# Keys and gathers of a graph-convolution kernel with matmuls of 256 columns in place of 512

## The reference, cut to what matters

```python
x_flat = x.reshape(B, C, N).transpose(0, 2, 1)          # B, C, N = 4, 128, 1024
emb = jnp.einsum('bnc,ec->bne', x_flat, dist_w)         # 32 wide
d2 = sq[:, :, None] + sq[:, None, :] - 2.0 * jnp.einsum('bne,bme->bnm', emb, emb)
_, idx = jax.lax.top_k(-dist, K)                        # K = 24
adj = (knn_mask & (dist <= THRESHOLD)) | jnp.eye(N, dtype=bool)[None]
S = (adj_f / De[:, None, :]) @ adj_f.transpose(0, 2, 1) / Dv[:, :, None]
out_flat = S @ X_lin + x_flat                           # then batch norm and SiLU
```

## Time and profile before

| | before |
|---|---|
| time, median of 3 runs | 173.44 us (173.38 to 173.76) |
| profiled execution, time | 173.33 us |
| profiled execution, span of the instructions | 171.5 us |
| TensorE matmul busy | 153.0 us, 89% |
| VectorE busy | 143.8 us, 84% |
| ScalarE busy | 118.5 us, 69% |
| GpSimd busy | 105.7 us, 62% |

### The profile page before, as it was taken

The page is one execution under the profiler, slowest core; times in us unless marked ns, Lnnn a source line. Parts: engine busy times, 40 slices in busy tenths (PEclk is TensorE's granted clock), DMA queues, the critical chain, the costliest instruction groups (busy, mean ns, idle before and its releaser), DMA issues.

```text
span 171.5 us, 4076 instructions
## 1 busy us (share of the span) xinstructions
PE 153.0 (89%) x1237; PEld 98.7 (58%) x1237; DVE 143.8 (84%) x863; ACT 118.5 (69%) x199; POOL 105.7 (62%) x160
## 2 busy tenths in 40 slices
PE   6999989899989999899999989999999899999000
PEld 2334523445556765566666757667877778979000
DVE  0676999999999894999999999599769986688582
ACT  1257679998696996985578799649916575590590
POOL 1000556869984677499996479999619999380000
PEclk9999999999999999999999999999999999999955
DMA  5821000406628666309726070980641369993057
GB/s 192 260 115 2 2 4 0 63 4 122 90 38 176 87 53 114 74 16 198 124 40 122 5 122 6 212 155 6 122 91 38 61 185 95 155 343 153 0 209 281
DMA packets 42346, 17.72 MB, mean 103 GB/s; under 512 B 38832, under 2 KB 39496, under 8 KB 42320
## 3 DMA queue, kind: packets, MB, share of 16 engines
q1 hardware_dynamic: 41456, 17.03, 47.3%
q10 hardware_dynamic: 864, 0.40, 0.9%
HBM read 6.11 MB, written 2.13 MB: 48 GB/s over the span
## 4 chain that ended last, share of the span: by engine, by line
PE 76%; ACT 6%; POOL 6%; DVE 6%; issue 4%; ACTq 0%; DVEq 0%; POOLq 0%
PE pt L500 23%; PE pg L474 21%; PE po L533 10%; PE pt L562 6%; PE po L453 3%; PE po L431 3%; PE pt L533 2%; PE po L440 2%; POOL x_wide L845 2%; DVE xn L1173 2%; ACT key L715 2%; POOL tw L837 1%; ACT xn L801 1%; PE pg L555 1%; PE pg L453 1%
## 5 line engine op out<-in xcount | busy, mean ns | idle before, releaser
L983 DVE MAX8 cand<-key 128x8 f32<-128x64 f32 x512 | 78.1, 208 | 1.4 <-ACT key L715 1.1
L500 PEld LDWEIGHTS pt<-xp,H 128*128 128x128 bf16 x768 | 44.4, 97 | 8.6 <-issue 7.6
L500 PE MATMUL pt<-xp,H 128*128 128x128 bf16 (+1 forms) x768 | 49.1, 220 | 0.0
L715 ACT ACTIVATE key<-pg 128x512 f32<-128x512 f32 x64 | 34.6, 594 | 19.1 <-PE pg L474 18.7
L474 PE MATMUL pg<-right,left 64*128 64x512 f32 x128 | 40.1, 641 | 2.4 <-ACT key L715 2.4
L882 POOL TENSOR_SCALAR H<-sign 128x1024 bf16<-128x1024 bf16 x32 | 33.4, 1044 | 13.1 <-ACT sign L723 13.1
L723 ACT ACTIVATE sign<-key,thr 128x1024 bf16<-128x1024 f32 x32 | 36.8, 1150 | 5.8 <-DVE thr L999 5.5
L474 PEld LDWEIGHTS pg<-right,left 64*128 64x128 f32 x128 | 12.4, 184 | 15.2 <-issue 7.1
L845 POOL CAST x_wide<-HT 128x1024 fp32r<-128x1024 bf16 x12 | 12.2, 1038 | 4.8 <-PE po L533 4.8
L562 PE MATMUL pt<-filler 128*128 128x512 bf16 x42 | 13.2, 443 | 1.3 <-POOL filler L806 1.3
L811 POOL TENSOR_SCALAR xn<-x_sb,gn_nm,gn_rs 128x1024 f32<-128x1024 f32 x3 | 3.6, 1194 | 16.3 <-DVE gn_rs L970 16.3
(11 more groups left out here) (96 smaller groups left out, 214.3 us busy)
## 6 DMA issues: line engine op xcount, KB each, us to landing
x_sb<-x SPq DMA_DIRECT2D x1, 2048.0 KB, 7.9
out<-xn SPq DMA_DIRECT2D x7, 256.0 KB, 2.2
dvb<-inv_rows SPq DMA_DIRECT2D x3, 512.0 KB, 4.3
x_sb<-x SPq DMA_DIRECT2D x1, 1024.0 KB, 6.4
left<-left SPq DMA_DIRECT2D x6, 128.0 KB, 2.3
x_sb<-x SPq DMA_DIRECT2D x1, 512.0 KB, 3.8
HT<-H SPq DMA_TRANSPOSE x32, 3.3
x_sb<-x ACTq DMA_DIRECT2D x1, 256.0 KB, 3.2
```

The costliest lines, as they stand in the source:

```text
L500: mm = pe.matmul(pt[:, j // T_BLOCKS, at:at + wide], lhs, x_cols(b, t, q, wide), start=(t == 0 and j % T_BLOCKS == 0 and q == 0), stop=(t ...
L715: act.activation(key[:, k % KEYS, cols], pg[:, h, :], ACT.Copy).then_inc(s["drained"], 1)
L983: ins = dve.max(cand[:, k % 2, c, :], key[:, k % KEYS, c * CHUNK:(c + 1) * CHUNK])
```

## The change

Each key matmul and each gather matmul of 512 columns becomes two of 256, with the same weights. In `fill_key` the order is columns 0 to 255 of both halves, then columns 256 to 511 of both halves; both banks' waits (and, in the first tile, both halves' operand waits) now stand ahead of the first matmul, and `filled` is signalled by the second piece of each half. In `gather` the two pieces of a matmul follow each other. Image 3's 256-wide parts stay as they are.

```diff
                     bank_free(p, h)
-                    rows = slice(h * SECOND, (h + 1) * SECOND)
-                    at = (t * P + (h * HALF if b > 0 else 0)) % N
-                    pe.matmul(pg[:, h, :], left[rows, b % 2, at:at + P], right[rows, b % 2, :],
-                              start=True, stop=True).then_inc(s["filled"], 1)
+                for a in (0, HALF // 2):
+                    for h in range(2):
+                        rows = slice(h * SECOND, (h + 1) * SECOND)
+                        at = (t * P + (h * HALF if b > 0 else 0)) % N
+                        mm = pe.matmul(pg[:, h, a:a + HALF // 2], left[rows, b % 2, at:at + P],
+                                       right[rows, b % 2, a:a + HALF // 2], start=True, stop=True,
+                                       skip_group_check=True)
+                        if a > 0:
+                            mm.then_inc(s["filled"], 1)
...
                     last = q == T_PIECES - 1 and j == TILES - 1
-                    mm = pe.matmul(out_bank(b, part), tw[:, q, j * C:(j + 1) * C], wide_cols(b, a // P, z // P, j),
-                                   start=(j == 0 and q == 0), stop=last, skip_group_check=True)
+                    for m in range(a, z, HALF // 2):
+                        mm = pe.matmul(out_bank(b, part)[:, m - a:m - a + HALF // 2], tw[:, q, j * C:(j + 1) * C],
+                                       wide_cols(b, m // P, (m + HALF // 2) // P, j),
+                                       start=(j == 0 and q == 0 and m == a), stop=last, skip_group_check=True)
                     if last:
                         mm.then_inc(s["o_ready"], 1)
```

## The result

The changed kernel takes 175.16 us (median of 6 runs, 174.87 to 176.33) against 173.41 us for the kernel before (173.12 to 173.76, 6 runs): a ratio of 1.0111, 95% interval 1.0084 to 1.0138. It is slower by 1.1%. The profiled execution took 175.01 us with a span of 173.1, 1.68 us more than the 173.33 of the one before. Forecast: 174.8 us, range 174.0 to 175.6.

The account below looks back on a forecast made before the run. TensorE was taken to bound the kernel up to 128 us and from 140.4 us, GpSimd between. Terms 0.67 + 0.27 + 0.46 = 1.40 us on the profiled 173.33 gave 174.73, as median 174.8 us, range 174.0 to 175.6.

Parts of the forecast that it names:

- start-up, h = 0 waiting with h = 1: First tiles' keys: h = 0 starts only with h = 1, delaying ScalarE's copies and then TensorE; +0.67 us (0 to 0.9).
- key's pieces: Key matmuls as four of 256 columns: 10 ns more a tile for 27 tiles, +0.27 us (0 to 0.54).
- gather's pieces: Gather matmuls split in two: 6 ns more for each of 80 on the path, +0.46 us (-1.4 to +0.8).
- The wait for both banks: Keys: both halves start when the second bank is free; TensorE loses only in the first tiles, +0.67 us.
- The later staggered keys cost nothing: Some eight later keys whose second bank comes free late: no cost, ScalarE being busy or banks asked for later.
- seam: Rival, between a key's pieces: second weight load exposed, about 0.19 us a tile, +5.1 us, 179.9; chance 0.05.
- The rival: Gather: alternating columns make pieces quicker, 17 ns saved a split, -1.4 us, total 173.0; chance 0.10.
- Absorbed: Rival: ScalarE catches up the start-up delay after tile 4, leaving +0.73 us, 174.2; chance 0.12.
- piled up: Rival, behind tile 4: key copies another 0.5 to 1 us late, TensorE waits for banks, 175.4 to 176; chance 0.09.

Follow-up runs that it names:

- half by half: The changed kernel with each half's two key pieces in succession behind that half's own waits: 173.89 against 173.27 us for the kernel before, ratio 1.0026.

## Why the prediction was right, and where not

The direction, the mechanism in the start-up and the range held, but one step failed, the second waits: 175.16 in 174.0 to 175.6, with 0.8% forecast and 1.1% measured. The terms, to tile 31 and behind it:

| term | forecast | measured |
|---|---|---|
| start-up, h = 0 waiting with h = 1 | +0.67 | +0.79 by tile 4 with a single bank wait (0.69 by tile 3) |
| a second bank wait at one matmul | not in the sum | +0.54 to tile 31, of which 0.09 by tile 4 |
| key's pieces | +0.27 | +0.13 (1.50 less 1.37; a key 1.064 for 1.059 us) |
| gather's pieces | +0.46 | +0.1 (-0.1 to +0.3) |
| sum | +1.40 | +1.68 profiled, +1.75 by medians |

The measured terms add up to 1.56, 0.1 to 0.2 short of the whole, which is within the interval of the gather's term.

*The wait for both banks.* Tile for tile as forecast to within 0.12 us in the first three, and passed on in full to 128 us; GpSimd's stretch then added nothing (1.56 before it, 1.58 behind). The run with each half's own waits took it away. (TensorE's chain isn't without a pause from 24 us on, as I had it: in the kernel before it passes through VectorE from 30.1 to 30.7 and through ScalarE from 45.3 to 49.7. Both follow TensorE there and were late with it, so no slack opened.) With a single bank wait TensorE was 0.69 us late by tile 3, against the forecast's 0.66. The 0.10 at tile 4 that makes it 0.79 comes with a wait too: h = 1, which had had its bank's wait alone, now stood behind the operand's as well.

*"The later staggered keys cost nothing": wrong.* This is the step that failed. Its reasoning on banks was right (with one wait and 512 columns, the shift grows by only 0.04 us from tile 5 to tile 31). But two bank waits in front of one matmul aren't one wait: I had asked when each half's wait is fulfilled, and put what a second wait costs TensorE at nothing. The price could have been read before the change, at tile 4 of the kernel before: 0.14 us from ScalarE's copy to the key there, 0.04 at tile 13. The shift grows by 0.1 at tiles 7, 12, 15, 19 and 27. At tile 13 it doesn't grow, though the 0.14 stands there: ScalarE's copies, which that key waits for, were 1.05 us late while TensorE was 1.15 late, so the added 0.1 only filled the difference.

*The key's pieces.* No seam, as the norms' rows had said; the price is in the lower part of the interval, 5 ns a tile. (The upper bound of 20 ns in the forecast took the 0.43 as 5 ns too high but left the 0.217, which comes from it, as it was; worked through, it is 13 ns.)

*The gather's pieces.* Mis-sized. I took the 0.119 us of the existing 256-wide parts for all of them. With `x_wide` that was right (0.118 to 0.119 us a piece, 0.232 a whole matmul: the forecast's 6 ns); with `wide_a` the pieces run at 0.114 and a split saves 2 to 4 ns. On the path the two nearly cancel. The rival named alternation as the cause, and that falls: the pieces alternate between the halves of a part in both, and only one of them got quicker. Its size (17 ns) was seen in neither. `wide_a` and `x_wide` also go with different PSUM banks of `po`, and which of the two makes the difference wasn't tried. (80 x 6 ns is 0.48 and not 0.46; the slip changes nothing.)

*Absorbed, or piled up.* Neither came. The copies of tile 4 were 1.3 us late, and those of tile 5 were again no later than TensorE.

The misses, some 0.5 us too much for the pieces of keys and gather and 0.54 us left out for second waits (0.66 with the start-up's 0.12), nearly cancelled. That the total fell so near the forecast is luck; the direction and the start-up term are not.

## What to carry to other kernels

When a loop is reordered so that several matmuls share a point of waiting, look first at the place of the waits, then at the matmuls: here nine tenths of the loss came with the matmuls unchanged. Where two waits on one counter meet, keep the higher one alone. A filler that keeps the clock up costs time where the engine is on the path: here ten in place of seventeen gained 0.4% at full clock, and leaving out all of them lost 0.3%, so try fewer before none. Before merging waits, look in the old trace for a matmul that already stands behind two of them and read its price there.

## What the runs showed that I had not expected

- A second wait on a matmul, fulfilled or implied, delays it by 0.06 to 0.1 us if one of the waits blocks (weight load 0.11 us behind the release in place of 0.05; first matmul 0.14 in place of 0.04 where both halves start together), and by nothing that shows if all waits are long fulfilled (1.06 us for a key in every run).
- Two f32 matmuls for rows 64 to 127 run beside those for rows 0 to 63 even when both of the latter stand ahead of them in the program (half by half, 1.14 us for eight records; with 0.43 us for a pass of 512 columns, the eight would take 8 x 0.215 = 1.7 us one after the other).
- Without fillers the granted clock fell to 0.50 for 6.8 us, after a stretch (28 to 32 us) in which TensorE was busy for 2.65 of 4 us; with ten fillers in place of seventeen TensorE was busy for 3.37 of them and the clock stayed at 1.00.
- The same split of a 512-column fp32r matmul in two saved 2 to 4 ns with one operand in SBUF and lost 5 to 6 ns with another, in another PSUM bank.
